# A graph attention layer with a mixture of experts: the router's logits made with nodes on partitions in one product, and one semaphore wait per tile for the counts' one-hots

## The reference

```
n = layernorm(x);  h = n @ W + b_w
e = leaky_relu(h@a[:512] [dst] + h@a[512:] [src] + b_a, 0.2);  w = exp(e)
x = x + segment_sum(w / segment_sum(w, dst)[dst] * h[src], dst)

n2 = layernorm(x);  logits = n2 @ Wg + bg;  probs = softmax(logits)
comb = probs where among the two largest, else 0
x = x + sum_e comb[:, e] * (gelu(n2 @ W1[e] + b1[e]) @ W2[e] + b2[e])
```

## Time and profile before

| what | us |
|---|---|
| median of 3 runs | 788.67 (786.93 to 788.84) |
| profiled execution, own time | 787.67 |
| its span | 786.0 |
| TensorE busy (share of the span), weight loads busy | 701.5 (89%), 527.0 |
| VectorE busy | 559.3 |
| ScalarE busy | 458.8 |
| GpSimd busy | 283.5 |

### The profile page before, as it was taken

The page is one execution under the profiler, slowest core; times in us unless marked ns, Lnnn a source line. Parts: engine busy times, 40 slices in busy tenths (PEclk is TensorE's granted clock), DMA queues, the critical chain, the costliest instruction groups (busy, mean ns, idle before and its releaser), DMA issues.

```text
span 786.0 us, 15439 instructions
## 1 busy us (share of the span) xinstructions
PE 701.5 (89%) x3556; PEld 527.0 (67%) x3557; DVE 559.3 (71%) x1520; ACT 458.8 (58%) x1226; POOL 283.5 (36%) x427
## 2 busy tenths in 40 slices
PE   3977863999899999999999999999589899999992
PEld 1855641777677776767677777776347788888881
DVE  4999977999888898879887888853495333333331
ACT  3223379778778776767676777721354455555551
POOL 3336620022222222222111222211305677777764
PEclk9888976999999999999999999999789999999998
DMA  9431000000000000000000000000793577777766
GB/s 337 158 107 55 0 1 1 15 29 28 28 27 3 28 27 28 27 28 27 28 27 28 27 12 17 27 28 28 245 407 112 103 130 133 133 128 135 135 119 80
DMA packets 28949, 59.70 MB, mean 76 GB/s; under 512 B 3664, under 2 KB 8144, under 8 KB 28624
## 3 DMA queue, kind: packets, MB, share of 16 engines
q0 software_dynamic: 10176, 24.12, 17.1%
q1 hardware_dynamic: 18704, 34.89, 12.0%
HBM read 35.93 MB, written 23.07 MB: 75 GB/s over the span
## 4 chain that ended last, share of the span: by engine, by line
PE 52%; DMA 10%; issue 5%; DVE 4%; POOL 2%; POOLq 2%; ACT 0%; DVEq 0%; ACTq 0%
PE ps L772 10%; PE ps L790 10%; PE ps L773 9%; DMA out_dram<-y,si 9%; PE ps L726 7%; PE ps L879 3%; PE ps L753 2%; PE ps L893 2%; PE ps L737 2%; PE ps L820 1%; DMA xg<-xn_table,gi 1%; PE ps L746 1%; PE ps L869 1%; PE ps L759 1%; DVE hot_r L1509 1%
## 5 line engine op out<-in xcount | busy, mean ns | idle before, releaser
L973 ACT ACTIVATE weight<-sdst_b,ss 128x125 f32 (+1 forms) x400 | 118.3, 386 | 95.5 <-DVE A_lo L1339 95.5
L772 PE MATMUL ps<-H_hi,A_hi 128*125 128x512 f32 x400 | 163.0, 408 | 0.9 <-DVE x_all L1353 0.9
L773 PE MATMUL ps<-H_lo,A_hi 128*125 128x512 f32 x400 | 157.9, 395 | 0.0
L1278 DVE TENSOR_SCALAR hot_k<-lane_k,key_t 128x250 bf16<-128x250 bf16 x600 | 120.6, 282 | 4.4 <-DVE weight_sum L1327 4.3
L524 POOL TENSOR_SCALAR seed<-seed 128x1 f32<-128x1 f32 x20 | 4.2, 210 | 330.9 <-DVE seed L1380 330.9
L982 ACT ACTIVATE weight<-weight,ss 128x125 f32<-128x125 f32 x400 | 119.8, 384 | 0.0
L790 PE MATMUL ps<-H_hi,A_lo 128*125 128x512 f32 x400 | 104.9, 402 | 0.0
L726 PE MATMUL ps<-hot_k,hot_l 128*128 128x250 bf16 x500 | 80.7, 286 | 16.0 <-DVE hot_k L1278 15.9
L772 PEld LDWEIGHTS ps<-H_hi,A_hi 128*125 128x125 f32 x400 | 74.2, 185 | 21.6 <-issue 3.7
L773 PEld LDWEIGHTS ps<-H_lo,A_hi 128*125 128x125 f32 x400 | 74.3, 186 | 16.1
L879 PE MATMUL ps<-W_e,xgT 128*128 x352 | 85.0, 385 | 0.0
(11 more groups left out here) (235 smaller groups left out, 1126.7 us busy)
## 6 DMA issues: line engine op xcount, KB each, us to landing
W_e<-in_L_ffn_W_dram SPq DMA_DIRECT2D x16, 512.0 KB, 9.3
xf<-in_x_cols_dram SPq DMA_DIRECT2D x10, 512.0 KB, 5.9
x_all<-in_x_dram SPq DMA_DIRECT2D x20, 256.0 KB, 5.8
out_dram<-x_all SPq DMA_DIRECT2D x20, 256.0 KB, 2.0
xn_table<-xn SPq DMA_DIRECT2D x20, 256.0 KB, 2.2
b_b<-in_L_ffn_b_dram SPq DMA_DIRECT2D x1, 2048.0 KB, 12.6
Wf<-in_L_gnn_W_dram SPq DMA_DIRECT2D x1, 1024.0 KB, 5.5
out_dram<-x_all POOLq DMA_DIRECT2D x4, 256.0 KB, 7.8
```

The source lines that it names most:

```text
L772: pe.matmul(ps_agg[0:TN, :], A_hi[:, k, :], H_hi[:, k, :], start=(k == 0), stop=False)
L773: m = pe.matmul(ps_agg[0:TN, :], A_hi[:, k, :], H_lo[:, k, :], start=False, stop=False)
L973: m = nc.scalar.activation(weight[:, s, k, :], dst_scores, ACT.Relu, bias=ss[:, 0, k:k + 1], scale=1.0 - SLOPE)
L1278: return nc.vector.tensor_scalar(into, lane_k[:, :], float(HW * h), key, ALU.add, ALU.is_equal)
```

## The change

The logits' product swaps its operands: xnT is stationary (128 nodes as columns), Wg with 8 columns moves, and the result comes out with nodes on partitions, directly in ps_nodes. The product moves from the A_hi products to the place where `logits_of_nodes` stood; that product, ScalarE's `logT_of` and their semaphores go. The bias is loaded to all partitions (bg_b) and added by VectorE to all logits at once ahead of the softmax. In `count`, steps whose t is in a register wait once for all ten halves ahead of the first product; the others still wait for each half.

```diff
-        logT = sb("logT", [NX, P], F32)
-        bg_c = sb("bg_c", [NX, 1], F32)
+        bg_b = sb("bg_b", [P, NX], F32)
...
-            sp.dma_start(bg_c[:, :], bg.rearrange("(e o) -> e o", o=1)).then_inc(ld_late, 16)
+            sp.dma_start(bg_b[:, :], bg.partition_broadcast(P)).then_inc(ld_late, 16)
...
+                at_once = not isinstance(t, int)
+                if at_once:
+                    pe.wait_ge(pairs_ok, HALVES * t + HALVES)
                 for h in range(HALVES):
-                    pe.wait_ge(pairs_ok, HALVES * t + h + 1)
+                    if not at_once:
+                        pe.wait_ge(pairs_ok, HALVES * t + h + 1)
...
             def normal_T(t, s):
                 pe.wait_ge(xn2_ok, t + 1)
-                if not (isinstance(t, int) and t < 1):
-                    pe.wait_ge(logT_ok, t)
...
             def logits(t):
                 pe.wait_ge(xnT_ok, t + 1)
                 for k in range(KT):
-                    m = pe.matmul(ps_T[0:NX, 0:P], Wg_sb[:, k, :], xnT[:, k, :], start=(k == 0), stop=(k == KT - 1))
-                m.then_inc(logT_ps, 1)
-            def logits_of_nodes(t):
-                pe.wait_ge(logT_ok, t + 1)
-                pe.matmul(ps_nodes[:, bass.ds(t * NX, NX)], logT[:, :], ident[0:NX, 0:NX], start=True, stop=True)\
-                    .then_inc(logit_ps, 1)
+                    m = pe.matmul(ps_nodes[:, bass.ds(t * NX, NX)], xnT[:, k, :], Wg_sb[:, k, :],
+                                  start=(k == 0), stop=(k == KT - 1))
+                m.then_inc(logit_ps, 1)
...
-                        if k == NT // 4 and has(t, 3):
-                            logits(t - 3)
...
                         if k == NT // 4 and has(t, 3):
                             pe.wait_ge(den_ok, t + 1)
-                            logits_of_nodes(t - 3)
+                            logits(t - 3)
...
                 if not (isinstance(t, int) and t < 1):
-                    act.wait_ge(logT_ps, t)
+                    act.wait_ge(logit_ps, t)
                 nc.scalar.activation(xnT[:, :, :], ps_T.rearrange("p (k n) -> p k n", k=KT), ACT.Copy).then_inc(xnT_ok, 1)
-            def logT_of(t):
...
-                if has(t, 3):
-                    logT_of(t - 3)
...
-            link(V.tensor_reduce(red[:, :], logit, AX.X, ALU.max))
-            V.tensor_tensor(score[:, :, :], logit, bc_t(red[:, :]), ALU.subtract).then_inc(shift_ok, 1)
+            link(V.tensor_tensor(score[:, :, :], logit, bg_b[:, :].unsqueeze(1).to_broadcast([P, NT, NX]), ALU.add))
+            link(V.tensor_reduce(red[:, :], score[:, :, :], AX.X, ALU.max))
+            V.tensor_tensor(score[:, :, :], score[:, :, :], bc_t(red[:, :]), ALU.subtract).then_inc(shift_ok, 1)
```

More of the change, by code:

```diff
@@ L314, in gnn_moe_kernel @@
         minus_ok = sem("minus_ok")
-        xnT_ps, xnT_ok, logT_ps, logT_ok, logit_ps = (sem(n) for n in (
-            "xnT_ps", "xnT_ok", "logT_ps", "logT_ok", "logit_ps"))
+        xnT_ps, xnT_ok, logit_ps = (sem(n) for n in ("xnT_ps", "xnT_ok", "logit_ps"))
         shift_ok, exp2_ok, cnt_ok, cnt_ps = sem("shift_ok"), sem("exp2_ok"), sem("cnt_ok"), sem("cnt_ps")
@@ L783, in tile_products @@
                                 .then_inc(den_ps, 1)
-                elif has(t, 3):
-                    logits(t - 3)
                 if has(t, 0):
```

## The result

| what | before | after |
|---|---|---|
| median | 788.46 (4 runs) | 801.97 (801.15 to 808.73, 4 runs) |
| ratio, 95% interval | | 1.0194 (1.0137 to 1.0251) |
| profiled execution, own time | 787.67 | 801.15 |
| its span | 786.0 | 799.5 |
| steps 4 to 17, from the add_x of tile 3 to that of tile 17 | 300.69 | 316.91 |

The forecast was 789.6 in a range of 784.5 to 795.5. The time lies outside it, on the slower side.

What follows compares the result with a forecast made beforehand. TensorE is busy 89%, but VectorE's den was taken to bound even steps and its loop-back branch odd ones. +2.2 + 0.56 - 1.0 - 0.9 = +0.9 on 787.67 gives 788.6; the median, 1.0 higher, 789.6; range 784.5 to 795.5.

Steps and rivals of the forecast that it cites:

- Even step: Loop, add_x to add_x: den after 16.22 us, products resume 1.08 later, 4.16 to next add_x; +0.31 each.
- A_lo products resume after den, even steps: TensorE in the loop: 0.20 us from den to first load plus 0.88 for the new product, 1.08; bounds 0.36 and 1.89.
- new product, loads 0.11 apart: Logits' product behind the wait for den: eight weight loads at 0.11 us each, 0.88; bounds 0.31 and 1.52.
- odd step without a fall: Loop's odd steps: new chain of 21.04 us stays under the 21.90 set by VectorE's loop-back branch, so 0.
- loop without the clock: Steps 4 to 17: seven even steps longer by 0.31 us each, odd steps and step 17 unchanged; +2.2.
- step 3: Ahead of the loop, den already awaited: logits' 0.37 us becomes 0.93 with the new product, +0.56.
- steps 18 and 19: Behind the loop, no one-hots to make, TensorE the bound: -0.48 us each, -1.0 together.
- after the last tile: Old logits chain gone, bias add added: score ready 1.4 us earlier, of which 0.9 taken to reach the end.
- rival A: New product's loads do not overlap, 0.19 us each, 1.52 in all, behind den: +7.3, 796.0; chance 0.13.
- B: Loop: den is in time, so TensorE's savings count until VectorE bounds a pair at 41.50 us: 777; chance 0.08.
- C: Odd steps' 2.9 us idle is a wait for TensorE, no branch price: -0.2 each, 788; chance 0.07.
- D: Ahead of the counts, the one wait for the one-hots is late: 0.6 us in 14 steps, +8.4, 797; chance 0.03.

Runs made afterwards that it cites:

- e4: Changed kernel with five needless products of 512 columns per tile put ahead of TensorE's wait for den: 791.32 us, ratio 1.0036.
- e5: Changed kernel with the new logits' product back among the A_hi products, behind the wait for the previous tile's den: 773.68 us.
- e3: Changed kernel with VectorE reading the denominator ahead of all one-hots instead of between their halves: 766.54 us.
- e9: Kernel of e3 with steps 4 to 17 written out as straight code instead of a loop: 761.56 us.
- e11: Changed kernel with two needless products of 512 columns per tile, instead of the five of e4, ahead of the wait for den: 794.90 us.
- e10: Kernel before with only the one wait per tile, old logits, and den read after seven of ten one-hot halves instead of five: 806.86 us.
- e1: Changed kernel with the ten waits per tile put back, the logits as changed: 797.91 us.

## Why the prediction was wrong, and where it was right

**The step that failed.** "So it stalls 0.5 to 2 us, all that both edits save is spent there", and then "Even step: 16.22 + 1.08 + 4.16 = 21.46". The stall came, in most steps at the upper end of that (1.87 in the odd steps, 1.35 to 2.58 in the even ones), and the terms of the even step are right to 0.1 us. But the 4.16 behind them is the time of 14 A_lo products and the transposes at full clock, taken from a kernel in which TensorE hardly stood still. Against 21.46, five even steps took 23.14 or 23.15 and two 24.48 or 24.49; two odd ones took 22.46 instead of 21.6. Measured by e4 this term is +16.0 us, and the sum had nothing for it. The prediction named the clock only for the stretch after 550 us, within a chance of 0.07, and the range held no part of it.

The rest of the sum, without the clock, measured in the profiled executions:

| step of the prediction | forecast | measured |
|---|---|---|
| A_lo products resume after den, even steps | 1.08 | 1.17 to 1.18 in after (where no fall came first), 1.07 to 1.08 in e4 |
| new product, loads 0.11 apart | 0.88 | 228.02 - 227.11 = 0.91 |
| even step without a fall | 21.46 | 21.43 to 21.47 (e4) |
| odd step without a fall | 21.90, unchanged | 21.60 to 21.74 |
| loop without the clock | +2.2 | +0.3 (e4) |
| step 3 | +0.56 | 20.76 - 20.20 = +0.56 |
| steps 18 and 19 | -1.0 | -0.62 - 0.77 = -1.4 |
| after the last tile | -0.9 (score -1.4) | -1.4 (exponential -1.3) |

*The loads* settle rival A: TensorE's weight loads in step 5 are eight in 0.97 us, and the next line's load begins 0.89 after the first.

```profile
249.53 0.97 PEld L753 LDWEIGHTS ps<-Wg_sb,xnT 128*128 128x128 f32 x8 [2.31 <-issue]
250.42 0.99 PEld L781 LDWEIGHTS ps<-H_hi,A_lo 128*125 128x125 f32 x5
```

*The loop* without the clock, as e4 has it, is 1.9 us better than forecast because five of the six odd steps gained 0.2 to 0.4 each (step 11 nothing) and step 17 0.35 (20.75 after 21.10). I had taken all of the odd step's 21.90 as fixed by VectorE; den came 15.63 after add_x instead of 15.81, and the step with it. *After the last tile* all of the earlier exponential reached the end, the upper end of what I had given. These rows answer to the earlier trace rows (transposes, new product, bias add, exponential, from the timelines of all engines):

```profile
571.30 1.11 PE L746 MATMUL ps<-ident,xn 128*128 128x128 f32 x4 [4.01 <-ACT xn L992]
573.10 1.87 PE L753 MATMUL ps<-Wg_sb,xnT 128*128 128x8 f32 x8 [0.69 <-ACT xnT L1000]
575.08 0.33 DVE L1434 TENSOR_TENSOR score<-ps,bg_b 128x160 f32<-128x160 f32 x1 [0.96 <-PE ps L753]
576.15 0.34 ACT L1030 ACTIVATE pr<-score 128x160 f32<-128x160 f32 x1 [3.11 <-DVE score L1436]
```

From the last add_x (564.08) to the exponential it is 12.07 us, before 562.59 - 549.19 = 13.40; from there to the end of the span nothing was lost. The product takes 1.87 instead of 1.05 because the clock is at its lower level there, as it was before the change.

All of it: the loop +0.3 and the clock +16.0, ahead of step 3 -0.5, step 3 +0.56, steps 18 and 19 -1.4, the end -1.4: +13.5, the whole difference of the spans. Without the clock it would have been -2.5 by these sums (an estimate; no run is the kernel after at full clock without added work), 3.4 us under the forecast's +0.9.

**The rivals.** A (1.52 us for the loads) did not happen. B (den in time) did not in the kernel as changed, but e5 and e3 brought it about, and both came out under its 777. C, that the idle time of odd steps is a wait for TensorE: in the kernel after add_x started 0.96 to 1.11 us behind TensorE's last product in the odd steps without a fall, 0.22 in even ones, and e9 took this away with the branch. (e9 also has constants in place of all waits against registers, but the even steps, with such waits, had only 0.22.) So it belongs to the loop-back. But its size is no constant: it was 2.8 to 3.1 us of VectorE's idle time here and 1.9 in e3.

The traces show what stands behind it. VectorE's queue takes the branch of the first round at 252.3 us in the kernel after and at 248.0 in e3:

```profile
L386 DVEq COMPARE_BRANCH  x7: 50/56/56, 252.3 to 525.3; - x7
L386 DVEq COMPARE_BRANCH  x7: 50/56/56, 248.0 to 490.0; - x7
```

About 1.0 us later one packet of 8 KB of the DMA kind "instruction" starts (the kernel after in the stretch 253.2 to 253.4, e3 in 249.0 to 249.2):

```profile
q14 instruction: 1, 0.01, 11.9%
q14 instruction: 1, 0.01, 12.5%
```

And add_x follows 2.1 us behind it in both (255.39 and 251.17). At each loop-back of every kernel with the loop where TensorE is not what add_x waits for, such a packet starts 2.1 to 2.3 us ahead of add_x; in e9 none stands at a fixed distance. So the time from branch to add_x is the same 3.1 to 3.2 us, and the idle time is what is left of it once the last one-hot has ended: the branch is taken 0.3 us ahead of that end in the kernel after, 1.2 in e3. This agrees with the fetch at a taken branch that the prediction cites. The packets name no engine, so that these are VectorE's is read from their times only.

D (the one wait late) did not show either (its 797 leaves out the forecast's own +0.9: from 789.6 it would be 798); from 211 to 512 us TensorE never stood ahead of the counts in the kernel after.

**What stays open.** Why the clock fell in nine of fourteen steps and not in the others, and whether the thin product has a part in it. Separated is only that the stall brings it (e4, e11), that it does so with the old logits too (e10), and what it costs.

## What to carry to other kernels

- Where TensorE waits for a value that is only just in time, time saved on TensorE becomes a stall, and the stall can lower its clock: give it a price of its own in the sum, the products behind the stall at half clock, and a rival with a chance of its own, even if the trace of before has no fall.
- Move the producer first. One line moved on VectorE (the read of the denominator, 3 us earlier) brought nothing that can be told to the kernel before and 35 us to the kernel after.
- To know whether a slower kernel suffers from the stall or from the clock, fill the stall with products that nobody needs. If more work makes it faster, it was the clock, as in e4.

## What the runs showed of the hardware that I had not expected

- The granted clock went from 1.00 to 0.50 at or shortly after waits of 1.35 to 2.6 us (in e1 from 1.14, in e11 from 1.33), with TensorE 91% busy over the stretch of 279 us in the kernel after. It cost 1.7 us in an even step with one short fall, 0.8 in an odd one, and 3.0 in the two steps where it stayed low for 6.8 us.
- 1.3 us of needless products per tile made the kernel 10.7 us faster.
- A stall of 2.72 us in step 3 had no fall in the kernel after, and in e1, with the same code in that step, the fall was there: the same place of the same code can go either way from kernel to kernel.
- VectorE's idle time at the loop-back was 2.8 to 3.1 us, or 1.9 with 30 one-hots in one run ahead of the branch. From the branch to the next add_x it was 3.1 to 3.2 us in both, with a packet of instructions on the way.
